# A transformer block on one core: GpSimd takes three more softmax-sum steps a unit, the attention output is multiplied in place in two buffers, and the first unit's operands are loaded during the projection

## The reference

```
h = layernorm(x) * (1 + ca) + sa
c_kv = h @ W_kv_down                      # 512 -> 128
k, v = c_kv @ W_k_up, c_kv @ W_v_up       # 16 heads of 32
q = h @ W_q
qr, kr = rope(h @ W_q_rope), rope(c_kv @ W_k_rope)    # 32 wide, shared by all heads
scores = (q k^T + qr kr^T) / 8, causal
x = x + ga * (softmax(scores) @ v) @ W_o
h = layernorm(x) * (1 + cb) + sb
x = x + gb * sigmoid(xr @ W_r^T) * (relu(xk @ W_k^T)^2 @ W_v^T)   # xr, xk mix h with the token before
```

## Time and profile before

| | |
|---|---|
| median of 3 runs | 4124.86 us (4112.24 to 4128.85) |
| the profiled execution, its own time | 4117.91 us |
| its span | 4116.2 us |
| mean granted TensorE clock | 0.952 |
| TensorE matmul busy | 3737.5 us, 91% |
| VectorE busy | 2840.8 us, 69% |
| GpSimd busy | 2436.3 us, 59% |
| ScalarE busy | 1789.5 us, 43% |

### The profile page before, as it was taken

The page is one execution under the profiler, slowest core; times in us unless marked ns, Lnnn a source line. Parts: engine busy times, 40 slices in busy tenths (PEclk is TensorE's granted clock), DMA queues, the critical chain, the costliest instruction groups (busy, mean ns, idle before and its releaser), DMA issues. The chain is left out here.

```text
span 4116.2 us, 57078 instructions
## 1 busy us (share of the span) xinstructions
PE 3737.5 (91%) x19808; PEld 2428.7 (59%) x19808; DVE 2840.8 (69%) x5454; ACT 1789.5 (43%) x3401; POOL 2436.3 (59%) x1145
## 2 busy tenths in 40 slices
PE   7999679889898899989999899889999699999998
PEld 4777445555555555555555555555555377777777
DVE  5777477767667677776777767767667277777776
ACT  2333235445454454544545445454455233333332
POOL 1333237666675676766766668666676555555555
PEclk9999889999999999999999999999999799999999
DMA  5888863462534534435345353362531211111110
GB/s 181 286 290 285 252 126 75 87 129 64 109 77 95 120 75 98 102 71 121 74 96 115 74 120 75 80 136 61 112 75 45 105 51 61 61 61 61 61 61 31
DMA packets 238409, 438.40 MB, mean 107 GB/s; under 512 B 25332, under 2 KB 26868, under 8 KB 238072
## 3 DMA queue, kind: packets, MB, share of 16 engines
q1 hardware_dynamic: 238136, 435.68, 41.2%
q10 hardware_dynamic: 64, 0.02, 0.0%
HBM read 300.86 MB, written 134.23 MB: 106 GB/s over the span
## 5 line engine op out<-in xcount | busy, mean ns | idle before, releaser
L800 ACT ACTIVATE att_probs<-att_ps_s 128x512 f32<-128x512 f32 (+3 forms) x2560 | 1304.0, 533 | 1414.7 <-PE att_ps_s L955 1306.8
L906 POOL TENSOR_TENSOR att_sum_g<-att_sum_g,att_probs 128x2048 f32<-128x2048 f32 (+3 forms) x384 | 1442.5, 3757 | 195.0 <-ACT att_probs L800 159.7
L836 DVE TENSOR_REDUCE att_piece_max<-att_ps_m 128x1 f32<-128x512 f32 x1536 | 994.2, 683 | 236.9 <-PE att_ps_m L940 230.7
L954 PE MATMUL att_ps_s<-att_q_a,att_k_a 128*128 128x512 f32 (+3 forms) x2560 | 963.3, 380 | 26.5 <-DMA att_q_b<-att_neg_max 24.7
L955 PE MATMUL att_ps_s<-att_q_b,att_k_b 65*128 65x512 f32 (+3 forms) x2560 | 939.3, 371 | 0.0
L940 PE MATMUL att_ps_m<-att_k_a,att_q_a 128*128 128x512 f32 (+3 forms) x1840 | 680.0, 395 | 183.6 <-DVE att_piece_max L839 130.7
L839 DVE CUSTOM_DVE_ANT_0 att_ps_m<-att_ps_m,mask_qk 128x128 f32<-128x128 f32 (+3 forms) x1024 | 490.5, 508 | 322.9 <-PE att_ps_m L940 314.8
L940 PEld LDWEIGHTS att_ps_m<-att_k_a,att_q_a 128*128 128x128 f32 x1840 | 346.3, 195 | 545.7 <-DVE att_piece_max L839 250.9
L961 PE MATMUL att_ps_o<-att_probs,att_v 128*32 128x512 f32 (+3 forms) x5120 | 620.2, 557 | 5.1 <-POOL att_probs L884 5.1
L954 PEld LDWEIGHTS att_ps_s<-att_q_a,att_k_a 128*128 128x128 f32 x2560 | 492.9, 193 | 160.8 <-issue 74.4
L955 PEld LDWEIGHTS att_ps_s<-att_q_b,att_k_b 65*128 65x128 f32 x2560 | 491.0, 192 | 68.5
(11 more groups left out here) (173 smaller groups left out, 5197.6 us busy)
## 6 DMA issues: line engine op xcount, KB each, us to landing
att_q_a<-s_q_hi SPq DMA_DIRECT2D x128, 256.0 KB, 6.5
att_q_a<-s_qr_hi SPq DMA_DIRECT2D x128, 256.0 KB, 7.3
prj_x_sb<-in_x_dram SPq DMA_DIRECT2D x16, 1024.0 KB, 5.3
s_q_hi<-prj_q_hi SPq DMA_DIRECT2D x16, 1024.0 KB, 4.4
s_q_lo<-prj_q_lo SPq DMA_DIRECT2D x16, 1024.0 KB, 6.4
s_k_hi<-prj_k_hi SPq DMA_DIRECT2D x16, 1024.0 KB, 6.7
s_k_lo<-prj_k_lo SPq DMA_DIRECT2D x16, 1024.0 KB, 7.6
s_v<-prj_v_sb SPq DMA_DIRECT2D x16, 1024.0 KB, 8.8
```

The costliest lines, as they stand in the source:

```text
L800: act.activation(probs[t % RING][:, hh, c0:CH], ps_s[(GH * t + hh) % SBANKS][:, c0:CH], ACT.Exp, scale=SCALE).then_inc(probs_ready, 1)
L836: dve.tensor_reduce(top, ps_m[:, bank, :], AX_X, ALU.max).then_inc(piece_taken, 1)
L906: pool.tensor_tensor(sum_g[:, :, c0:CH], sum_g[:, :, c0:CH], new, ALU.add).then_inc(sum_added, 1)
L954: mm(out[:, c0:CH], k_a[:, hh, i * P:(i + 1) * P], q_a[j][:, hh, c0:CH], start=True, stop=False)
```

## The change

Four things:

1. `SHARE_OF` gives GpSimd three more steps of each unit (step 0 of the diagonal in block 1; in block 2 the fourth step; in block 3 two `T` in place of three, at steps 6 and 12 of the block). TensorE's ones-matmul has seven steps a unit instead of ten.
2. `o_raw` is gone. ScalarE copies `ps_o` into one of two `o_sb` and VectorE multiplies it in place. ScalarE's copy waits for the store of two blocks before; the multiply waits for no store. SP's order in `body` changes: the old unit's last store comes first, and each block's store before the next maxima row.
3. Rotary rows are stored once a chunk, not four times, and the attention loads read them from there.
4. The operand buffers of the first unit are allocated before the projection (which reuses two raw weight buffers for its own tiles to make room). SP's projection program is written out for all 16 chunks instead of a loop, and issues after chunks 6 to 13 the loads of unit 0: all of `k_a`, `q_a` of blocks 0 and 1, `v`, and `q_b` of block 0. The rest is loaded at the start of attention, that of blocks 2 and 3 only after the first maxima row has been placed.

```diff
-        xn = sb("xn", [P, TB, D], F32)
+        xn, up_raw = prj["weights"][2][0], prj["weights"][4][0]
...
-        rot_a, rot_b = sb("rot_a", [DR, 2, CH], F32), sb("rot_b", [DR, 2, CH], F32)
+        rot_a, rot_b = up_raw[0:DR, :, :], sb("rot_b", [DR, 2, CH], F32)
...
                 for j in range(2):
-                    sp.dma_start(to_r[0][j][n], as_f32(rot[0][:, j, None, :]).broadcast_to([DR, NG, CH])).then_inc(st_r, 16)
+                    sp.dma_start(to_r[0][j][n], as_f32(rot[0][:, j, :])).then_inc(st_r, 16)
...
-            with sp.Fori(0, NCH - 2) as n:
-                body(n, True, True)
-            body(NCH - 2, False, True)
-            body(NCH - 1, False, False)
+            load_q_a, load_q_b, load_k_a, _, load_v, _ = operand_loads(sp, scratch, ops)
+            early = [lambda: load_k_a(0, 0), lambda: load_q_a(0, 0), lambda: load_k_a(0, 1), lambda: load_q_a(0, 1),
+                     lambda: load_k_a(0, 2), lambda: load_k_a(0, 3), lambda: [load_v(0, j) for j in range(TCH)],
+                     lambda: load_q_b(0, 0)]
+            for n in range(NCH):
+                body(n, n < NCH - 2, n < NCH - 1)
+                if FIRST_EARLY <= n < FIRST_EARLY + len(early):
+                    early[n - FIRST_EARLY]()
...
-SHARE_OF = ("TTTT", "GGGGTGGG", "GGGTGGGGTGGG", "GGGTGGGTGGGGTGGG")
+SHARE_OF = ("TTTT", "GGGGGGGG", "GGGGGGGGTGGG", "GGGGGGTGGGGGTGGG")
...
+    def rotary(a, i):
+        return scratch[a][i % NCH][:, None, :].broadcast_to([DR, GH, CH])
...
-        o_raw, rden, o_sb = (sb(n, [P, CH], F32) for n in ("o_raw", "rden", "o_sb"))
+        rden, *o_sb = (sb(n, [P, CH], F32) for n in ("rden", "o_sb0", "o_sb1"))
...
             def body(u, nxt):
+                if u:
+                    store_o(u - 1, TCH - 1)
                 if nxt:
                     load_k_next(u + 1)
                     wait_alone(sp, scores_ready, GH * (NSTEP * u + STEPS[0]), sp_mark)
                     load_q(u + 1, 0)
-                if u:
-                    store_o(u - 1, TCH - 1)
-                for j in range(1, TCH - 1):
-                    place_max(u, j + 1)
-                    store_o(u, j - 1)
-                    if nxt:
-                        wait_alone(sp, scores_ready, GH * (NSTEP * u + FIRST[j] + STEPS[j]), sp_mark)
-                        load_q(u + 1, j)
-                store_o(u, TCH - 2)
+                store_o(u, 0)
+                place_max(u, 2)
+                if nxt:
+                    wait_alone(sp, scores_ready, GH * (NSTEP * u + FIRST[1] + STEPS[1]), sp_mark)
+                    load_q(u + 1, 1)
+                store_o(u, 1)
+                place_max(u, 3)
+                if nxt:
+                    wait_alone(sp, scores_ready, GH * (NSTEP * u + FIRST[2] + STEPS[2]), sp_mark)
+                    load_q(u + 1, 2)
+                store_o(u, 2)
...
-            for j in range(TCH):
-                load_k_a(0, j)
+            load_k_b(0, 0)
+            load_k_b(0, 1)
+            load_q_b(0, 1)
+            wait_alone(sp, m_in[0], 16, sp_mark)
+            for j in range(2, TCH):
                 load_q(0, j)
                 load_k_b(0, j)
-                load_v(0, j)
...
             def take_output(u, j):
                 act.wait_ge(pv_done, NSTEP * u + FIRST[j] + STEPS[j] + RING)
-                act.wait_ge(o_ready, TCH * u + j + 1)
-                act.copy(o_raw[:], ps_o[:]).then_inc(o_copied, 1)
+                if TCH * u + j >= 2:
+                    act.wait_ge(o_stored, 16 * (TCH * u + j - 1))
+                act.copy(o_sb[j % 2][:], ps_o[:]).then_inc(o_copied, 1)
...
-                waits(dve, (rden_ready, TB * (TCH * u + j + 2)), (o_copied, TCH * u + j + 2), (o_stored, 16 * (TCH * u + j) + 1))
-                dve.tensor_tensor(o_sb[:], o_raw[:], rden[:], ALU.mult).then_inc(o_ready, 1)
+                waits(dve, (rden_ready, TB * (TCH * u + j + 2)), (o_copied, TCH * u + j + 2))
+                dve.tensor_tensor(o_sb[j % 2][:], o_sb[j % 2][:], rden[:], ALU.mult).then_inc(o_ready, 1)
...
-        scratch[a] = scratch_of("s_" + a, (slots, DR, CH))
+        scratch[a] = scratch_of("s_" + a, (NCH, DR, CH))
```

More of the change, by code:

```diff
@@ L209, in projection_buffers, with projection @@
     return prj
-def projection(nc, keep, dram, scratch, prj):
+def projection(nc, keep, dram, scratch, prj, ops):
     with ExitStack() as ctx:
@@ L603, in attention @@
         sem = lambda n: ctx.enter_context(nc.semaphore("att_" + n))
-        k_a = sb("k_a", [P, GH, T], F32R)
+        k_a, v = ops["k_a"], ops["v"]
         k_b = sb("k_b", [2 * HD + 1, GH, T], F32R)
-        q_a = [sb(f"q_a{j}", [P, GH, CH], F32R) for j in range(TCH)]
-        q_b = [sb(f"q_b{j}", [2 * HD + 1, GH, CH], F32R) for j in range(TCH)]
-        v = sb("v", [P, TCH, TB, P], F32)
+        ops["q_a"] += [sb(f"q_a{j}", [P, GH, CH], F32R) for j in range(2, TCH)]
+        ops["q_b"] += [sb(f"q_b{j}", [2 * HD + 1, GH, CH], F32R) for j in range(1, TCH)]
+        q_a, q_b = ops["q_a"], ops["q_b"]
         probs = [sb(f"probs{i}", [P, GH, CH], F32) for i in range(RING)]
@@ L621, in attention @@
         ps_m = ctx.enter_context(nc.psum_tensor("att_ps_m", [P, MBANKS, CH], F32))
[L623 to L625 removed]
+        q_in, k_in, qb_in, v_in = (ops[n] for n in ("q_in", "k_in", "qb_in", "v_in"))
         kb_in = [sem(f"kb_in{j}") for j in range(TCH)]
[L627 removed]
         m_in = [sem(f"m_in{j}") for j in range(TCH)]
@@ L696, in _ @@
         def _(sp):
-            heads = {a: scratch[a].rearrange("n (h r) t -> n r h t", h=GH) for a in ("q_hi", "q_lo", "k_hi", "k_lo")}
-            def rotary(a, i):
-                return scratch[a][i][:, None, :].broadcast_to([DR, GH, CH])
+            load_q_a, load_q_b, load_k_a, load_k_b, load_v, (heads, rotary) = operand_loads(sp, scratch, ops, k_b, kb_in)
             def load_q(u, j):
[L703 to L717, removed]
-                for row, src in ((0, heads["k_hi"][i]), (HD, rotary("kr_hi", i))):
-                    sp.dma_start(as_f32(k_b[row:row + HD, :, j * CH:(j + 1) * CH]), src).then_inc(kb_in[j], 16)
+                load_q_a(u, j)
+                load_q_b(u, j)
             def load_k_next(u):
@@ L1465, in adaln_block @@
         }
-        with ExitStack() as first:
-            prj = projection_buffers(nc, first)
-            setup(nc, keep, dram, scratch, prj)
-            projection(nc, keep, dram, scratch, prj)
-        attention(nc, keep, scratch)
+        with ExitStack() as held:
+            ops = operands(nc, held)
+            with ExitStack() as first:
+                prj = projection_buffers(nc, first)
+                setup(nc, keep, dram, scratch, prj)
+                projection(nc, keep, dram, scratch, prj, ops)
+            attention(nc, keep, scratch, ops)
         feedforward(nc, keep, dram, scratch, out)
```

45 lines of the change are left out of this document (36 added, 9 removed).

## The result

The changed kernel takes **3937.02 us** (median of 4 runs, 3933.77 to 3938.36) against 4123.64 us (4112.24 to 4128.85) for the kernel before on the same chip: a ratio of 0.955 with a 95% interval of 0.9529 to 0.9571. The forecast was 3918 in a range of 3888 to 3975. The profiled execution took 3938.36 us, its span 3936.6, at a mean granted clock of 0.972.

The account below looks back on a forecast made before the run. Attention bounds: TensorE sets the pace but stops for VectorE's maxima, delayed by the output tile's store. Terms -140 - 39 - 2 + 5 - 27 = -203 against 4117.9 us gave 3915, stated as 3918, range 3888 to 3975.

Parts of the forecast that it names:

- Part 1: Attention, steps 8 and 9 of 14 units: output multiplied in place in two buffers, store issued first; -139.6 us.
- the second maxima row: Start of attention: its 8.46 us wait meets a shorter queue as SP holds 16 loads back; -4 to -8, taken -7.
- Part 2: Attention: three full-width ones-matmul groups a unit fewer on TensorE, 0.87 us each; -39 us, and -2 in unit 15.
- stall-free unit: Unit 15 of the old kernel, steps 8 and 9: 9.42 us at clock 1.00, the multiply's wait for GpSimd included.
- The doubt about steps 10 and 17: VectorE leaves at most 1.25 us free there, so the gain from removed ones-matmul groups could be as low as nothing.
- Part 3: The same three steps as sums on GpSimd: 0 in units 0 to 14, +5 us in unit 15.
- the first rival: GpSimd becomes the bound: its chain late by one sum in blocks 1 and 2, 142 us back, 4060 us; 8%.
- Part 4: Projection and start of attention: first unit's operands loaded early, rotary rows stored once; together -27 us (-20 to -33).
- A stall moved to the next DMA: Attention: block 2's maxima row or queries late instead; up to 129 us, 4047 us; 6%.
- The store still waited for: Attention: wait remains through ScalarE's copy or SP reaching the store late; at most half of the -139.6 back, 3988 us; 3%.
- A slow projection: Early loads slow the projection, 3.7 us in each of 8 chunks, 29 us in all: 3944 us; 8%.
- The port lost to the next sum as well: Multiply at three closes a unit loses the SBUF port to another GpSimd sum: 291 us, 4206 us, slower; 3%.

Follow-up runs that it names:

- Part 1 alone: Kernel before with two output tiles multiplied in place, ScalarE's copy waiting for the store of two blocks before, and SP's new order: 3994.66 us, ratio 0.970.

## Why the prediction was right

The sum was -203 us on the profiled execution; -179.6 came. The mechanisms were the ones named, and no rival took place. The missing 24 us are roughly 12 in part 1, where a clock loss was left out, 6 at the second maxima row, 6 in the feed-forward stage and 1 in part 2, less 2 by which the first score was earlier still.

- **Part 1** (-139.6). Steps 8 and 9 gave -133.0. "It is the changed kernel's stall-free unit, run inside the old one" held to 0.03 us in ten units. In the other four the clock falls to 0.84, not the 1.00 that was to show it right, and they take 10.8 us: the term left out that the 1.3 us pause which stays in step 8 can cost clock. Step 28, where nothing was changed, took 5.4 us more: the clock falls behind its 1.8 us pause in ten units, in the old kernel it did so in seven (7.3 us or more against 6.2), and by less. Part 1 alone shows the same (-131.7 and +6.9). ScalarE's wait for the store costs nothing, as forecast: there is no such row in the waits. SP's new order, which the prediction moved along at no gain of its own, is a second cure for the same stall.
- **Part 2** (-39, of it 36.5 in units 1 to 14). The step table has -35.5. The doubt about steps 10 and 17 was needless: they give the full 0.86 us, though VectorE is busy 2.82 of 3.02 and 4.29 of 4.71 us in the rows above. (Of the "steps 4 and 15" whose groups run there, the first is counted within block 1; in the unit it is step 8.)
- **Part 3** (0, and +5 in unit 15). No wait for GpSimd before unit 15. Unit 15 as a whole is +2.9, for -2 + 5. GpSimd is busy 232 us more; 220 were worked out, and its sums are a little longer now, 4629 ns against 4585. The chain worked for block 1 was close: it gave 1.0 and 1.6 us for the clear of step 10 and the close, and unit 2 has 1.2 and 1.8. But it did not look at the clear of step 9, which is the tightest with 0.7. Block 2 had 3.7 us to spare, and a fourth sum there made the first rival true in part.
- **Part 4** (-20.5 and -7). The first score came 22.3 us earlier. (A drain that ends at 489.4 and shortens by 2.6 is over at 486.8, not 487.4; the first maxima stand at 485.34.) The projection keeps its pace, 26.17 us a chunk. **The step that failed is the second maxima row**: "it meets a shorter queue: -4 to -8, I take -7". It waited 8.82 us, before it was 8.46. The queue was not shorter: SP's 16 held-back loads moved at 205 GB/s, and behind them SP had already issued the next unit's first keys and six query loads, which the prediction did not count. With both held back the row comes 6.6 us earlier, as the experiment shows.
- **Feed-forward** (0): +6.3 us with its code untouched. In the other executions profiled its matmuls span 841 to 851 us; before it was 839.7, after 846.5. The code is the same in all of them, so this is the difference from one execution to another, as far as is known, and the old profile had the shortest. A term of 0 there is uncertain by some 6 us or more.
- **Where the sum was placed.** I placed the sum on an execution of 4117.9 us and added 3 for the median. The kernel before had a median of 4123.64 beside the change. The gain is 186.6 us between the medians and 179.6 between the spans, so the sum was 16 to 24 us too large either way.

**The rivals.** GpSimd as the bound: no, by 0.7 us in block 1 and by less than one sum in block 2. A stall moved to the next DMA: in units 1 to 15 nothing waits for the row due at step 12, and the one at step 24 is waited for by 0.3 us on average, as before. The store still waited for: no. A slow projection: no; a chunk that now has an early load beside it shows DMA at 296 GB/s for 285 and takes 26.17 us. The port lost to the next sum as well: at most 3.69 us for a multiply in units 1 to 15, and 4.67 once in unit 0, where it started just behind the start of a sum; a second sum would have made it over 7. (Its price has a slip: 10.6 us for 7.8 of wait is a clock loss of 2.8 us and not 1.5, which fits the 9.3 us of the other seven units; with 2.8 it would be 354 us and not 291.)

The prediction names the multiply's wait for GpSimd inside its 9.42 us, but only asks whether it may shift; it takes the old stall-free unit for the floor. The wait is worth 1.6 us of TensorE's time there, and the ends of blocks 1 and 2 hold 1.4 and 2.1 more, in the kernel before too (steps 16 and 28 are no shorter there). With the clock that they cost they are worth 100 us in the changed kernel, more than parts 2 to 4 together.

## What to carry to other kernels

A wait for a store of an output tile can be cured from either end: issue the store ahead of the loads, or give the tile a second buffer. One of them is enough, so look which one costs nothing. When a stall-free stretch is taken as the model for the stretch with the stall, look inside it for what still waits: an operation four times its shortest duration is such a place. And a pause of a microsecond on TensorE is worth more than itself when the granted clock falls behind it; price both.

## What was not expected of the hardware

- The clock after a short pause is not the same from unit to unit. Behind the same 1.8 us in step 28, after the same matmuls, TensorE is at 1.00 in some units and at 0.78 in others (6.2 and 7.6 us), within one execution; behind 1.3 us in step 8 it is so in four units of 14 in one kernel and in ten in another that differs only in unit 0 and unit 15. Where the pauses are gone (the kernel with the denominators in PSUM) all 14 units agree within 0.02 us in steps 8, 16 and 28.
- With 16 DMA engines busy all the time the loads of attention's first operands move 205 GB/s, where the projection's drain moved 305. The cause was not looked for.
- GpSimd's queued sums give a waiting multiply its turn between two of them, in each of the 46 cases in the stretch shown where a sum is beside it: the longest multiply is 3.69 us where two sums would be over 9. The next sum starts some 0.15 us behind the last one, before the multiply has ended, and takes 4.8 us and not 4.6.
